# Attention layer with experts on one core: Q, K and V by seven block products in place of eight from the second batch on

## The chip, the core and the metric

The kernel runs on one core of a Trainium2 chip. The metric is device time in microseconds (us) of one execution; lower is better. The engines are named as in the profile: PE is TensorE, DVE VectorE, ACT ScalarE, POOL GpSimd, and SP the queue that only issues DMAs.

## The reference, cut to what matters

x is 4 batches of 1024 rows of 512. The layer is attention with 16 heads of width 128, a residual and a layer norm, then a router with 32 experts and a shared expert, a residual and a layer norm. The change is in the attention alone:

```python
qkv = einsum('bsh,hf->bsf', x, w_qkv)              # 512 -> 3 * 16 * 128
scores = einsum('bhqd,bhkd->bhqk', q, k) / sqrt(128)
probs = softmax(scores, axis=-1)
values = einsum('bhqk,bhkd->bhkd', probs, v)       # = v times the column sums of probs
out = values @ w_o                                 # then layernorm(x + out)
```

The second einsum with probs has no sum over different rows of v: each key's row of v is multiplied by the column sum of the probabilities.

## The kernel before

There are 64 heads in all (4 batches by 16), M in the code. They are worked in 32 pairs, `pair(i)`; n is the head whose scores are made, and in the same eight steps t the projections of head n + 1 are made. Every float32 matrix is kept as a rounded part (HI) and a rest (LO), and a product is three passes, HI*HI, HI*LO and LO*HI. One matmul instruction takes a 128 x 128 weight and 512 columns.

- PE, step t: `scores(n, t)` is 6 matmuls into one of two score banks pairs; it waits for `act_e`, the exponential of step t-2. Then in steps 0 to 5 `project(n + 1, g)` makes one of six groups (Q, K and V, each in two halves of 512 columns), 12 matmuls each, into one of the two banks `p_g`. `spread` (4 matmuls) lies in step 2; in steps 6 and 7 lie two `out_tile` each (6 matmuls each), which multiply the previous pair's values with w_o.
- DVE, step t: `max_tile` (L1325) on the scores, then the extras (`lo_g` L1347, `lo_cs` L1354, `times_v` L1363, `lo_val` L1368, `add_y` L1375), then `add_tile` of the step before (L1332, L1340).
- ACT, step t: first the casts to HI that stand in that step (`hi_g` L936, `hi_w` L907, `hi_cs`, `hi_val`, `hi_wo`, `hi_x`), then `exp_tile` (L953).
- POOL: `lo_w` (L640), `lo_wo` (L645) and `lo_x` (L652), the rests of the weights and of the next batch's x, behind ACT's casts.
- SP: loads of the raw weights and of x pieces, each 256 KB.

Each engine runs its instructions in the written order, and semaphores alone tie the engines together. After the last pair come the router, the shared expert and the experts; the change leaves them as they are, but for the place where some of their inputs come from.

## Time and profile before

| | |
|---|---|
| median of 3 runs | 2753.79 us (2751.57 to 2754.13) |
| profiled execution | 2753.52 us, span 2751.8 us |
| granted TensorE clock, mean | 0.997 |
| PE busy | 2730.4 us, 99% |
| DVE busy | 2162.6 us, 79% |
| ACT busy | 1407.3 us, 51% |
| POOL busy | 655.0 us, 24% |
| DMA | 193.51 MB, mean 70 GB/s |

The span is the time from the first to the last instruction; the execution's own time is 1.7 us more. A busy share is a mean over the attention (up to about 2165 us) and the rest. Matmuls overlap each other, so their spacing is read from the starts in the timeline and not from the length of one.

### The profile page before, as it was taken

Reading aid. Unit: us, or ns where it says so; the run is one execution under the profiler, and the core shown is the slowest. Engines: PE = TensorE matmul, PEld = TensorE weight load, DVE = VectorE, ACT = ScalarE, POOL = GpSimd, SP = SyncE. Lnnn points to the kernel's source line nnn. Section 1 sums busy time; section 2 is a strip of 40 time slices with the busy share of each in tenths; the row PEclk is TensorE's granted clock in tenths of the full one; section 3 lists DMA queues with packets and bytes.
Section 4 is the critical chain, followed back from the end, with each engine's and each line's share of the span. In section 5 each row is a group of like instructions: output and inputs, shape, how many; then the busy total and the mean of one; then the engine's idle time right before and its main releaser. Section 6 shows DMA issues by size and latency. Waiting matters only on the chain.

```text
span 2751.8 us, 41729 instructions
## 1 busy us (share of the span) xinstructions
PE 2730.4 (99%) x13008; PEld 2262.2 (82%) x13008; DVE 2162.6 (79%) x3193; ACT 1407.3 (51%) x2501; POOL 655.0 (24%) x690
## 2 busy tenths in 40 slices
PE   9999999999999999999999999999999999999998
PEld 7888888888888888888888888888888788888887
DVE  5988888888888888888888888888888787533346
ACT  5555555566555555665555557555555532244434
POOL 2221112222111211222112212212221110266520
PEclk9999999999999999999999999999999999999999
DMA  3111111113111111131111112211111231288954
GB/s 119 39 35 35 37 34 34 34 34 115 35 34 34 34 35 41 33 112 35 35 38 34 34 34 65 80 38 34 34 34 35 85 119 42 88 251 248 256 161 153
DMA packets 209639, 193.51 MB, mean 70 GB/s; under 512 B 14620, under 2 KB 162076, under 8 KB 209552
## 3 DMA queue, kind: packets, MB, share of 16 engines
q1 hardware_dynamic: 199056, 180.47, 20.7%
q0 software_dynamic: 10496, 12.02, 2.3%
q8 instruction: 38, 0.62, 0.1%
q14 instruction: 49, 0.40, 0.0%
HBM read 166.41 MB, written 36.18 MB: 74 GB/s over the span
## 4 chain that ended last, share of the span: by engine, by line
PE 96%; DVE 3%; issue 1%; ACT 1%; DMA 0%; DVEq 0%; ACTq 0%
PE banks L1789 37%; PE banks L1804 25%; PE banks L1827 13%; PE banks L1711 6%; PE banks L1760 5%; PE banks L1773 3%; PE banks L1720 2%; PE banks L1814 2%; PE banks L1635 1%; PE banks L1747 1%; DVE colsum L1340 1%; PE banks L1688 0%; PE banks L1659 0%; DVE neg_max L1325 0%; DVE rows_b L1363 0%
## 5 line engine op out<-in xcount | busy, mean ns | idle before, releaser
L1789 PE MATMUL banks<-xt,w_sb 128*128 (+1 forms) x4608 | 1109.1, 390 | 6.6 <-DVE xt L1419 6.6
L953 ACT ACTIVATE rows_a<-banks,neg_max 128x1024 f32<-128x1024 f32 x512 | 572.4, 1118 | 891.1 <-DVE neg_max L1325 890.7
L1789 PEld LDWEIGHTS banks<-xt,w_sb 128*128 128x128 f32 x4608 | 866.6, 188 | 187.4 <-POOL w_sb L640 6.6
L1325 DVE TENSOR_REDUCE neg_max<-banks 128x1 f32<-128x1024 f32 x512 | 625.9, 1222 | 282.5 <-PE banks L1804 279.6
L1804 PE MATMUL banks<-qk 128*128 128x512 f32 x3072 | 780.5, 390 | 0.5 <-ACT rows_a L953 0.5
L1804 PEld LDWEIGHTS banks<-qk 128*128 128x128 f32 x3072 | 576.9, 188 | 121.5 <-ACT rows_a L953 1.7
L1340 DVE SCALAR_TENSOR_TENSOR colsum<-rows_a,inv,colsum 128x1024 f32<-128x1024 f32 x448 | 586.8, 1310 | 18.8 <-DVE inv L1332 1.5
L640 POOL TENSOR_TENSOR w_sb<-raws,w_sb 128x512 fp32r<-128x512 f32 x192 | 257.9, 1343 | 1197.8 <-ACT w_sb L907 1197.8
L1827 PE MATMUL banks<-wo_sb,val 128*128 128x512 f32 x1536 | 372.1, 391 | 0.6 <-DVE y_sb L1375 0.6
L1827 PEld LDWEIGHTS banks<-wo_sb,val 128*128 128x128 f32 x1536 | 285.9, 188 | 67.3 <-DVE y_sb L1375 8.0
L645 POOL TENSOR_TENSOR wo_sb<-wo_raw,wo_sb 128x512 fp32r<-128x512 f32 x64 | 96.7, 1512 | 415.1 <-ACT wo_sb L913 415.1
L1711 PE MATMUL banks<-xt 128*128 128x512 f32 x768 | 184.4, 396 | 0.4 <-DVE rows_c L1304 0.4
L936 ACT ACTIVATE qk<-banks 128x512 fp32r<-128x512 f32 x256 | 152.7, 597 | 58.9 <-PE banks L1789 58.9
L1347 DVE SCALAR_TENSOR_TENSOR qk<-banks,qk 128x512 fp32r<-128x512 f32 x256 | 174.4, 681 | 5.6 <-ACT qk L936 5.6
L1711 PEld LDWEIGHTS banks<-xt 128*128 128x128 f32 x768 | 144.4, 190 | 31.0 <-issue 0.9
L1375 DVE TENSOR_TENSOR y_sb<-y_sb,banks 128x512 f32<-128x512 f32 x256 | 163.9, 680 | 4.1 <-PE banks L1827 4.0
L907 ACT CAST w_sb<-raws 128x512 fp32r<-128x512 f32 x192 | 118.1, 615 | 2.0 <-DMA raws<-in_w_qkv 2.0
L704 POOL DMA_INDIRECT acc_rows<-rows_b,who x64 | 94.1, 1471 | 87.1 <-DMA acc_rows<-rows_b,who 43.7
L880 ACT ACTIVATE rows_b<-banks,slot_w 80x512 f32<-80x512 f32 x64 | 43.6, 684 | 124.4 <-PE banks L1773 78.7
L1368 DVE TENSOR_TENSOR val<-rows_b,val 128x1024 fp32r<-128x1024 f32 x64 | 100.9, 1577 | 0.9 <-ACT val L947 0.9
L652 POOL TENSOR_TENSOR xt<-raws,xt 128x128 f32 (+1 forms) x128 | 80.7, 662 | 83.4 <-ACT xt L921 83.4
L1320 DVE TENSOR_TENSOR ehb<-ehf,ehb 128x320 fp32r<-128x320 f32 x32 | 15.7, 492 | 106.2 <-ACT ehb L875 106.2
(191 smaller groups left out, 2279.9 us busy)
## 6 DMA issues: line engine op xcount, KB each, us to landing
raws<-in_w_qkv SPq DMA_DIRECT2D x192, 256.0 KB, 2.9
wo_raw<-in_w_o SPq DMA_DIRECT2D x64, 256.0 KB, 2.8
y_sb<-in_x SPq DMA_DIRECT2D x32, 256.0 KB, 4.0
raw_own<-in_w_gate SPq DMA_DIRECT2D x16, 512.0 KB, 5.5
raw_own<-in_w_up SPq DMA_DIRECT2D x16, 512.0 KB, 5.7
raw_own<-in_w_down SPq DMA_DIRECT2D x16, 512.0 KB, 7.0
raws<-in_xT SPq DMA_DIRECT2D x25, 256.0 KB, 3.0
x_wide<-y_sb SPq DMA_DIRECT2D x24, 256.0 KB, 3.6
```

The lines of the kernel that those rows point to most:

```text
L640: pool.tensor_tensor(w_sb[:, LO, r], w_raw[:, r], rounded(w_sb[:, HI, r]), ALU.subtract)\
L936: act.activation(qk[:, par, r, HI, at], p_g[:, g % 2], ACT.Copy, scale=SCALE if r == Q else 1.0).then_inc(act_g, 1)
L953: act.activation(ex[:, t % 2], p_s[:, t % 2], ACT.Exp, bias=neg_max[:, t % 2], accum_out=rowsum[:, t % 2]).then_inc(act_e, 1)
L1325: dve.tensor_reduce(neg_max[:, t % 2], p_s[:, t % 2], AX_X, ALU.max, negate=True)\
L1340: dve.scalar_tensor_tensor(out=colsum[:], in0=ex[:, t % 2], scalar=inv[:, t % 2], in1=colsum[:], op0=ALU.mult, op1=ALU.add).then_inc(dve_p, 1)
L1347: dve.scalar_tensor_tensor(out=qk[:, par, r, LO, at], in0=p_g[:, g % 2], scalar=SCALE if r == Q else 1.0, in1=rounded(qk[:, par, r, HI, at ...
L1375: dve.tensor_tensor(y_sb[:, j], y_sb[:, j], p_o[:, j % 2], ALU.add).then_inc(dve_y, 1)
L1711: ins = pe.matmul(p_f(f % 2, r), s_gu[:, a, k, at], parts[:, PARTS_OF[u], b, k], start=(k == 0 and (a, b) == PASSES[0]), stop=(k == KC - 1 ...
L1760: ins = pe.matmul(expert_hidden(e, r)[:, ic * C_SLOTS:(ic + 1) * C_SLOTS], gate_up_of(e)[:, r, k, cols(ic)], exT[:, e % 2, k], start=(k == ...
L1789: ins = pe.matmul(p_g[:, g % 2], w_sb[:, a, r, c], xt_part(batch_par, b, c, half * NB, NB), start=(c == 0 and (a, b) == PASSES[0]), stop=( ...
L1804: ins = pe.matmul(p_s[:, t % 2, keys], qk[:, par, Q, a, at], qk[:, par, K, b, keys], start=((a, b) == PASSES[0]), stop=((a, b) == PASSES[-1]))
L1827: ins = pe.matmul(p_o[:, j % 2], val2[:, r, a, at], wo_sb[:, r, b], start=(r == 0 and (a, b) == PASSES[0]), stop=(r == 1 and (a, b) == PAS ...
```

## The change

**What it does.** A product of a matrix of 2 x 2 blocks with another is made from seven block products of sums of blocks (Strassen's method in Winograd's form). The blocks are two of the weights' columns (Q and K of a head, or V of two heads) by two halves of the depth 512, and two halves of depth by two halves of a batch's 1024 rows. A block product is `multiply`: 6 matmuls. Seven of them replace four groups of 12.

- In the first batch (pairs 0 to 7, `plain_head`) the projections are made as before. Beside it the sums for the later batches are made: per pair three sets of weights (`land_w`, `scale_new_w`, `combine_w`, `hi_new_w`, `low_w`, `store_w`), seven blocks of 256 words in two parts, and a piece of the next batch's x (`land_x`, `combine_x`, `hi_new_x`, `low_x`, `store_x_form`). They are stored in device memory. All the sets pass through one place in SBUF, `w_new`.
- From head 16 on (`quick`, and the second half of `turnover`, pair 7) a set of seven weights is read back per product: three per pair, each in two loads (`load_values`, `load_even`, `load_odd`) that POOL issues, 128x2048 and 128x1536 words, 1 MB and 0.75 MB. At a batch's end seven x blocks, 7 MB, are read back too (`load_x_form`).
- The results of the seven products are put together by ACT (`keep_q`, `keep_v`: a copy of the bank), DVE (`sum_q`, `sum_v`: bank plus a tile in SBUF) and POOL (`sum_q`, `sum_v`: two tiles in SBUF). `lo_q` and `lo_val` go to POOL; `lo_g` and `hi_w`, `lo_w` end with the first batch.

The lines of it that matter for the order (ACT in the first batch, SP at the start and at the end of a plain pair, POOL and PE in a quick one):

```diff
+        def land_w(first, second, count):
+            on_sp.wait_ge(out_w_form, 16 * count)
...
+        def store_w(at, count):
+            on_sp.wait_ge(pool_new_w, count + 1)
...
+        def plain(i):
...
+            land_piece(b, i)
+            if is_first(i):
+                land_w((Q, 1), (K, 1), 1)
+            store_w(n + 1, 3 * i + 1)
+            land_w((V, n), (V, n + 1), 3 * i + 2)
+            load_w(n + 3, n + 3)
+            store_w(H + i, 3 * i + 2)
+            store_piece(b, i)
+            land_w((Q, n + 2), (K, n + 2), 3 * i + 3)
+            store_w(n + 2, 3 * i + 3)
+            land_w((Q, n + 3), (K, n + 3), 3 * i + 4)
...
+        def scale_new_w(count):
+            on_act.wait_ge(in_new_w, 64 * (count + 1))
...
+        def plain_head(i, s):
...
+                if s == 0 and t == 0:
+                    scale_new_w(3 * i + 1)
+                if s == 1 and t == 4:
+                    scale_new_w(3 * i + 3)
+                if s == 0 and t == 1:
+                    hi_new_w(3 * i + 1)
...
+                if s == 1 and t == 6:
+                    hi_new_w(3 * i + 3)
+                exp_tile(n, t)
...
+        def load_values(b, i, part):
+            on_pool.wait_ge(pe_g, G * H + FORMS * (2 * i + 1 - H) + LOADS[part][1])
+            load_w_form(H + i - PB * b, part)
...
+        def multiply(bank, k):
+            for c in range(2):
+                for a, b in PASSES:
+                    ins = pe.matmul(p_g[:, bank], w_form[:, k, a, c], x_form[:, k, b, c],
+                                    start=(c == 0 and (a, b) == PASSES[0]), stop=(c == 1 and (a, b) == PASSES[-1]))
...
+        def product_v(i, k):
+            m = 2 * i + 1
+            on_pe.wait_ge(in_w_form[LOAD_OF[k]], 16 * (w_load(i, "values") + 1))
...
         def scores(n, par, t, quickly=True):
+            if t in (0, 4) and quickly:
+                on_pe.wait_ge(pool_w, 3 * H + 8 * (n - H) + (6 if t == 0 else 8))
+        def first_head(i):
...
+                if t == 0:
+                    product_q(i, 0, 0)
+                    product_q(i, 0, 1)
...
+                if 4 <= t <= 6:
+                    product_v(i, 2 * (t - 4))
+                    product_v(i, 2 * (t - 4) + 1)
```

**ACT at the start.** These rows stand around the first exponentials, those of head 0; L953 before and L1317 now is `exp_tile`. Before:

```order
L932 COPY v_sb<-banks 128x512 x2
L907 CAST w_sb<-raws 128x512
L953 ACTIVATE rows_a,rowsum<-banks,neg_max 128x1024
L936 ACTIVATE qk<-banks 128x512
L953 ACTIVATE rows_a,rowsum<-banks,neg_max 128x1024
```

Now, at the same place (L1226 is `scale_new_w`, L1230 `hi_new_w`, L1240 `hi_new_x`):

```order
L1296 COPY v_sb<-banks 128x512 x2
L1215 CAST w_form<-raws 128x512
L1226 ACTIVATE xt_words<-xt_words 128x2x256
L1230 CAST xt<-xt_words 128x7x256
L1240 CAST xt<-xt_words 128x7x128
L1226 ACTIVATE xt_words<-xt_words 128x2x256
L1317 ACTIVATE rows_a,rowsum<-banks,neg_max 128x1024
L1300 ACTIVATE qk<-banks 128x512
L1230 CAST xt<-xt_words 128x7x256
L1317 ACTIVATE rows_a,rowsum<-banks,neg_max 128x1024
```

Ahead of the first exponential now stand the whole of set 0, piece 0 of x, and the scaling of set 1.

**POOL in a quick pair.** These rows are the begin of pair 9; L859 is `sum_q`, L874 `lo_val`, L846 `lo_q`, L772 a weight load, L765 `lo_wo`. Before, POOL's work of a pair was six L640, two L645 and one piece of x.

```order
L859 TENSOR_TENSOR qk_words<-qk_words,raws 128x512
L874 TENSOR_TENSOR val<-rows_b,val 128x1024
L846 TENSOR_TENSOR qk<-qk_words,qk 128x512
L772 DMA w_form<-w_forms 128x2048
L859 TENSOR_TENSOR qk_words<-qk_words,raws 128x512
L765 TENSOR_TENSOR wo_sb<-wo_words,wo_sb 128x2x512
L859 TENSOR_TENSOR qk_words<-qk_words,raws 128x512
L772 DMA w_form<-w_forms 128x1536
```

The first L772 here loads the weights of the first four V products, which PE wants in step 4 of this head.

**PE in a quick pair.** These rows are steps 0 to 4 of the first head; L2366 is `scores`, L2317 a block product (6 matmuls, or 12 for two), L2376 `spread`:

```order
L2366 MATMUL banks<-qk 128x512 x6
L2317 MATMUL banks<-xt,w_form 128x512 x12
L2366 MATMUL banks<-qk 128x512 x6
L2317 MATMUL banks<-xt,w_form 128x512 x12
L2366 MATMUL banks<-qk 128x512 x6
L2317 MATMUL banks<-xt,w_form 128x512 x6
L2376 MATMUL banks<-cs,ones 128x512 x4
L2366 MATMUL banks<-qk 128x512 x6
L2317 MATMUL banks<-xt,w_form 128x512 x12
L2366 MATMUL banks<-qk 128x512 x6
L2317 MATMUL banks<-xt,w_form 128x512 x12
```

Before, a group of 12 stood in each of steps 0 to 5; now steps 0 to 7 hold two, two, one, two products of Q and K and then two, two, two, one of V.

## Rows read from the trace of the kernel before

**Rows 1.** The page: the chain that ended last, by engine and by line.

```profile
PE 96%; DVE 3%; issue 1%; ACT 1%; DMA 0%; DVEq 0%; ACTq 0%
```

**Rows 2.** Timeline of PE in a middle pair: start us, us, instructions.

```profile
1299.96 1.52 PE L1804 MATMUL banks<-qk 128*128 128x512 f32 x6
1301.32 2.88 PE L1789 MATMUL banks<-xt,w_sb 128*128 x12
1304.04 1.07 PE L1814 MATMUL banks<-cs,ones 128*128 128x512 f32 x4
1304.95 1.52 PE L1804 MATMUL banks<-qk 128*128 128x512 f32 x6
1306.31 2.88 PE L1789 MATMUL banks<-xt,w_sb 128*128 x12
1309.03 1.52 PE L1804 MATMUL banks<-qk 128*128 128x512 f32 x6
```

**Rows 3.** Busy time in a pair's 67.2 us: PE, PEld, DVE, ACT, POOL.

```profile
1299.00:1366.20 67.20, 67.20 (x297) 55.47 (x297) 57.53 (x73) 35.18 (x61) 13.66 (x13) 1.00 0.12 35
```

**Rows 4.** Timeline of DVE and ACT in the same pair, steps 3 and 4.

```profile
1306.51 1.23 DVE L1325 TENSOR_REDUCE neg_max<-banks 128x1 f32<-128x1024 f32 x1 [0.64 <-PE banks L1804]
1307.65 0.68 DVE L1347 SCALAR_TENSOR_TENSOR qk<-banks,qk 128x512 fp32r<-128x512 f32 x1
1307.77 1.12 ACT L953 ACTIVATE rows_a<-banks,neg_max 128x1024 f32<-128x1024 f32 x1 [2.42 <-DVE neg_max L1325]
1308.25 1.27 DVE L1363 TENSOR_TENSOR rows_b<-v_sb,banks 128x512 f32<-128x512 f32 x2
1308.79 0.19 ACT L953 ACTIVATION_READ_ACCUMULATOR rows_a<-banks,neg_max 128x1 f32 x1
1309.63 1.28 DVE L1340 SCALAR_TENSOR_TENSOR colsum<-rows_a,inv,colsum 128x1024 f32<-128x1024 f32 x1
```

**Rows 5.** Timeline of the start of the kernel: SP, PE and ACT.

```profile
18.33 4.09 SPq L500 DMA_DIRECT2D y_sb<-in_x  x8
26.73 0.62 ACT L907 CAST w_sb<-raws 128x512 fp32r<-128x512 f32 x1
28.87 1.12 ACT L953 ACTIVATE rows_a<-banks,neg_max 128x1024 f32<-128x1024 f32 x1 [1.51 <-DVE neg_max L1325]
34.21 1.52 PE L1804 MATMUL banks<-qk 128*128 128x512 f32 x6
```

**Rows 6.** Groups by line and shape over the span: xcount, busy us, mean ns.

```profile
L640 POOL TENSOR_TENSOR w_sb<-raws,w_sb 128x512 fp32r<-128x512 f32 x192 | 257.9, 1343 | 1197.8 <-ACT w_sb L907 1197.8
L743 POOL TENSOR_TENSOR qk<-raw_own,qk 128x1024 fp32r<-128x1024 f32 x2 | 4.8, 2376 | 8.8 <-ACT qk L901 8.8
L907 ACT CAST w_sb<-raws 128x512 fp32r<-128x512 f32 x192 | 118.1, 615 | 2.0 <-DMA raws<-in_w_qkv 2.0
L947 ACT CAST val<-rows_b 128x1024 fp32r<-128x1024 f32 x64 | 67.0, 1047 | 1.4 <-DVE rows_b L1363 1.4
```

**Rows 7.** DMA issues: KB each, median us from issue to landing.

```profile
raws<-in_w_qkv SPq DMA_DIRECT2D x192, 256.0 KB, 2.9
out_rows<-y_sb SPq DMA_DIRECT2D x2, 1024.0 KB, 4.7
out_rows<-y_sb SPq DMA_DIRECT2D x2, 512.0 KB, 2.8
rows_a<-x_wide SPq DMA_DIRECT2D x3, 1024.0 KB, 5.0
x_wide<-dense POOLq DMA_DIRECT2D x8, 64.0 KB, 2.2
```

**Rows 8.** Timeline of DVE and POOL where both work: the same L1368 twice.

```profile
1303.26 1.22 DVE L1368 TENSOR_TENSOR val<-rows_b,val 128x1024 fp32r<-128x1024 f32 x1
1304.39 0.16 DVE L1332 RECIPROCAL inv<-rowsum 128x1 f32<-128x1 f32 x1
...
1315.51 1.30 POOL L640 TENSOR_TENSOR w_sb<-raws,w_sb 128x512 fp32r<-128x512 f32 x1 [3.45 <-ACT w_sb L907]
1315.81 2.08 DVE L1368 TENSOR_TENSOR val<-rows_b,val 128x1024 fp32r<-128x1024 f32 x1
```

**Rows 9.** PE's one pause in the attention, timeline, then windows with the clock.

```profile
2138.26 1.33 PE L1635 MATMUL banks<-ident,rows_c 128*128 128x128 f32 x8 [2.04 <-DVE xt L1171]
2139.24 2.91 PE L1804 MATMUL banks<-qk 128*128 128x512 f32 x6
2141.94 1.41 PE L1814 MATMUL banks<-cs,ones 128*128 128x512 f32 x4
...
2139.20:2142.00 2.80, 2.80 (x10) 2.22 (x9) 2.60 (x4) 2.13 (x4) 0.00 (x0) 0.51 0.00 0
```

More of the change, by code:

```diff
@@ L1422, in _ @@
             lo_g(0, 0, g)
-        pairs(dve, pair)
+        pairs(dve, plain, turnover, quick)
         add_tile(M - 1, T - 1)
-        add_y(PAIRS - 1, 6)
         add_y(PAIRS - 1, 7)
@@ new lines, in plain_head @@
+        def plain_head(i, s):
+            n = 2 * i + s
+            for t in range(T):
+                scores(n, s, t, quickly=False)
+                g = group_at(i, t)
+                if g is not None:
+                    project(n + 1, 1 - s, g)
+                if t == 2 and not (is_first(i) and s == 0):
+                    if not is_first(i):
+                        on_pe.wait_ge(dve_y, T * (i - 1) if s == 0 else T * (i - 1) + 4)
+                    spread(n - 1)
+                if t >= 6 and not is_first(i):
+                    if t == 6:
+                        on_pe.wait_ge(dve_v, 2 * n)
+                    out_tile(i, 4 * s + 2 * (t - 6))
+                    out_tile(i, 4 * s + 2 * (t - 6) + 1)
```

946 lines of the change are left out of this document (721 added, 225 removed).

## The prediction

> **What bounds the kernel now.** I read the chain that ended last first: 96% of it is PE [rows 1]. Then a middle pair in PE's timeline: scores start at 1299.96, the group at 1301.32, so 6 matmuls take 1.36 us; the next scores after group and spread start at 1304.95, those after at 1309.03, 4.08 us for 18 matmuls [rows 2]. One matmul costs 0.2267 us and nothing lies between them. A pair has 296, which is 67.1 us. In the same stretch DVE is busy 57.5 us, ACT 35.2, POOL 13.7 [rows 3]. So PE sets the time of every pair, DVE has some 9.6 us of room, POOL more than 50. The timeline of DVE and ACT gives the slack of a step: the scores that start at 1304.95 are reduced from 1306.51, their exponential runs from 1307.77 to 1308.98, 4.0 us after the scores' start [rows 2, 4]. PE wants it two steps later, at 8.16 us. An exponential may be some 4.1 us late before PE stands.
>
> **What the change takes off PE.** Four groups of 12 matmuls become seven of 6: 6 fewer for each of 48 heads' Q and K and for each of 24 pairs' V, 432 matmuls. At 0.2267 us that is **-97.9 us**, all of it on the path as long as PE stays packed. A quick pair is 278 matmuls, 63.0 us.
>
> **Prices of the new operations.** POOL: 512 columns 1.29 us uncontended (the row of L640 in rows 8; its mean is 1.34), 1024 columns 2.38 [rows 6, 8], so 2.1 ns per column: 256 columns 0.74, 1792 columns 4.05. ACT: 512 columns 0.615, 1024 columns 1.05 [rows 6], so 1792 columns 1.7. A store of 1.75 MB: 512 KB took 2.8 us and 1024 KB 4.7 [rows 7], so estimated 6.7 (1.5 to 1.9 for each further 512 KB). Four loads of 128 KB: one of 256 KB lands in 2.9 us, and the fourth issue comes later by some 1.3, so 4.2. A load of 1 MB that POOL issues: the row has 64 KB in 2.2 us there and 1024 KB in 5.0 on SP [rows 7]; I take 5.1. The operation is in no trace; its bounds are 4.0 and 8.
>
> By the Trainium skill ("DMA: Bandwidth & Descriptors", Anatomy of one DMA, SWDGE path) such a load takes an estimated 2.0 us and the bytes at 436 GB/s, 4.4 us for 1 MB. By it the wait priced below would be 0.7 us shorter in each of 24 pairs, 17 us in all. The rows go before it, since they are of this kernel's own tiles, and no row here shows a large load from POOL.
>
> **The start.** Before, the first exponential starts at 28.87 and PE goes on without a gap [rows 5]. Now ACT's queue has set 0, piece 0 and the scaling of set 1 ahead of it. Laid end to end: loads of y occupy SP to 22.4 and their 2 MB must move first, set 0 lands near 29.5, scaling 0.6, four dependent POOL sums 3.3, cast 1.7, POOL's rest 4.05 (behind piece 0's sums) to 39.5, store to 46.5. Piece 0 (3584 rows of 256 B) is stored behind it, to 50; SP then lands piece 1 (its wait stands first) and set 1, to 57. The first exponential starts at 58, 29 us late; less the 4.1 of slack PE stands 25 us. Set 1's sums hold the second exponential in the same way for some 2 more. **+27 us**, and the clock: after PE's one pause of 2.04 us the next 6 matmuls took 2.7 us in place of 1.36, with a granted clock of 0.51, the 1.2 GHz level [rows 9]. 3.4 us at half rate cost 1.7. **+1.7**. Behind ACT here stand the exponentials and so all of PE and DVE; nothing else covers it.
>
> **Pairs 1 to 7.** All three sets of a pair pass through one place, so a set cannot land before the last is stored. The third set is cast in step 6 of the second head, 0.6 + 1.7 us behind its begin; then POOL 4.05, store 6.7, loads 4.2, scaling 0.6: set 4 is scaled 17.9 us after that step began. Step 0 of the next pair begins 8.16 after it and its exponential would start 2.8 later, at 10.96. It is 7.0 late, 2.9 more than the slack. The four sums then hold the second exponential (4.5 us with one DVE operation in between): another 1.4. **+4.3 us in each of 7 pairs, +30**. If the store and loads are 3 us quicker, 1.3 a pair; if DVE and the other transfers hold them, 7. The other two sets fit: their casts come later than their loads.
>
> **Quick pairs: the V weights.** In the first head POOL does the first sum (at 5.4 to 6.7 us of the pair, behind `keep_q` of product 1), then `lo_val`. That needs ACT's `hi_val`, which stands in step 2 behind the exponential of step 1 (to 8.3), a copy and a cast of 0.6 each and itself 1.05: 10.6. `lo_val` 2.4 to 13.0, then DVE's sum takes its turn (1.0), `lo_q` to 15.3, and only then the load is issued; it lands at 20.5. PE has three steps of 4.08, less 0.45 in step 2, and 1.36 of scores: it wants product 0 of V at 17.2. It stands **3.3 us, in 24 pairs +79**. Its cover would be later work of PE, but the order is fixed and the next scores are behind it. The second load lands by 28.5, when PE, now late, wants it. I do not count the clock's fall here: 1.7 us each time, 41 in all, is kept for the range, for the pause is near the only one that the trace shows.
>
> **Quick pairs: DVE and POOL.** DVE loses eight L1347 (0.60 by start to start, [rows 4]) and two L1368 (1.13, [rows 8]), and gets nine sums of 0.60: 57.5 - 4.8 - 2.3 + 5.4 = 55.8 us, and the contention of POOL. POOL gets per pair twenty operations of 512 columns, three of 1024, 2.1 for a piece's rest and four small: 25.8 + 7.1 + 2.1 + 1.8 = 36.8 us, and six issues of about 0.8. L1368 took 1.22 alone and 2.08 where POOL's L640 was under way, until which it did nothing [rows 8]. I call those DVE operations that read two tiles of SBUF exclusive against POOL: per pair 14 L1340, 2 L1337 and 2 L1354, 21.9 us. Both together need 58.7 of the 66 us, so it fits but DVE is often late by one POOL operation. Head for head that shows where slack is small: K's last `lo_q` must be done before the next pair's scores. ACT casts it behind the exponential of step 6, 0.6 us into step 7, POOL needs 1.3, and step 7 is but 2.72 long: 0.8 of slack. I take a wait of 0.3 us in 24 pairs, **+7**; bounds 0 and 1.5.
>
> The rule against this change is in the Trainium skill ("SBUF — State Buffer", two separate sides): the port pair that VectorE and GpSimd share is an exclusive lock, held for the whole instruction. By that rule the sum of both engines' lock time, not either's busy share, is the measure; it is the rival of VectorE's port below. The trace agrees in L1368's 2.08 us.
>
> **Batch openings and the end.** At the ends of batches 1 and 2 (pairs 15 and 23) 8.75 MB are issued by POOL from about 33 us of the pair, and PE wants the last of them 19 us later; at the 3.1 us per MB that the 1024 KB row leaves after 2 us of latency they take 27. Products spread over the steps cover most: **+6 each, 12**. The 14 small POOL operations of a norm stand ahead of the K chain three times, 2 each, **+6**. 4 MB for the shared expert are issued late in the last pair: **+3**.
>
> **The sum.** -97.9 + 27 + 1.7 + 30 + 79 + 7 + 12 + 6 + 3 = +67.8. From the profiled execution's own 2753.5 that is 2821; it stands 0.3 under the median, so **2822 us** against 2753.8.
>
> **Rivals.**
> - *The loads are in time (faster).* If the V weights land by 17.2 + 0.5 us and the sets' circle is 3 us quicker, what is left is -97.9 + 28.7 + 9 + 12 + 7 + 12 = -29: 2725; without the openings' waits 2710. For it: PE has no other new dependency in step 4. Against it: `hi_val` at 10.6 and `lo_val` at 13.0 stand on measured rows. It decides where the wait is under 0.5 us per pair. Chance 0.20.
> - *VectorE's port.* If POOL and DVE get in each other's way more than their turns fit, each exclusive DVE operation waits half a POOL operation, 18 x 0.65 = 11.7 us, DVE needs 67.5, and with in-order waits of ACT on POOL's results 70 per pair: 24 x (70 - 67.1) + 59 + 21 = +150, 2903. For it: 58.7 of 66 us. Against it: DVE catches up while PE stands. Chance 0.12.
> - *Half clock after each wait.* As the forecast, and each 3.3 us pause costs 1.7 more: 2863. For it rows 9, against it that a shorter pause may not lower the clock. Chance 0.20.
> - *It cancels.* Waits of 0.8 us per quick pair: within 0.2%. Chance 0.04.
> - The forecast: 0.44.
>
> 0.2% (5.5 us) is about what a measurement of this kernel can tell from no change. Faster is the first rival, 0.20; same 0.04; the rest slower, 0.76. The range goes to the first rival's half and to the port's case: 2722 to 2900. The forecast's own range is 2785 to 2850.
>
> **What would show it.** In the changed profile: 12576 matmuls; the first exponential (L1317) near 58 us; in pairs 1 to 7 ACT's L1226 waiting for a DMA and PE's scores for ACT, pairs of about 71.4 us; in quick pairs a pause of L2317 in step 4 with a DMA as its releaser, issued by L772, pairs of about 66.6; clock under 1 after it or not. Wrong would be: no pause at step 4 (then faster), or DVE's L1340 with a mean well over 1.5 us and DVE without idle time (then the port).

## The result and the profile after

The changed kernel takes **2995.05 us** (median of 4 runs, 2992.64 to 2996.57) against 2753.96 for the kernel before in the same rounds: a ratio of 1.088 (1.086 to 1.090), 241 us slower. The forecast was 2822 with a range up to 2900: right in its sign, 173 us short in its size.

The page of the changed kernel: the chain that ended last by engine, then three groups of operations (xcount, busy us and mean ns, idle time before them and its releaser):

```profile
PE 47%; issue 22%; POOL 10%; DVE 10%; DMA 6%; ACT 3%; SPq 2%; DVEq 1%; POOLq 0%; ACTq 0%
...
L1774 DVE SCALAR_TENSOR_TENSOR colsum<-rows_a,inv,colsum 128x1024 f32<-128x1024 f32 x448 | 903.2, 2016 | 17.6
L2317 PE MATMUL banks<-xt,w_form 128*128 128x512 f32 x3024 | 787.4, 409 | 103.4 <-DMA w_form<-w_forms 79.0
L2366 PE MATMUL banks<-qk 128*128 128x512 f32 x3072 | 791.8, 394 | 45.4 <-ACT rows_a L1317 35.1
```

PE's share of the chain fell from 96% [rows 1] to 47%; L1774 is DVE's `add_tile`, whose mean was 1310 ns before over the same 448 operations. PE waited 79.0 us for loads of weights, the number that the forecast has for it, and yet that is a third of the loss only.

Where the 241 us lie is read from the starts of `spread` (L2376), which stands once in every head at the same place. The table gives the time from the spread in one pair's second head to that in the next pair's, named by the first of the two:

| | before | after | sum of the difference |
|---|---|---|---|
| first spread | 65.5 | 92.7 | +27.2 |
| pair 0 | 61.8 | 78.2 | +16.5 |
| pairs 1 to 7 | 67.2 | 74.3, the last 76.7 | +52 |
| pairs 8, 16, 24 (norm of the batch before) | 67.6 | 85.3, 85.4, 84.5 | +52 |
| the 20 other distances between quick pairs | 67.2, the last 64.4 | 70.9 to 71.0 in nine, 69.8 to 74.3 in the others | +87 |
| the rest | | | +6 |

A middle quick pair, the same views as [rows 2 to 4]. First the windows: the pair, PE's pause in it, and what follows the pause (length, then busy us of PE, PEld, DVE, ACT, POOL, the granted clock, DMA share, GB/s). Then the timelines of PE, POOL and DVE:

```profile
1504.30:1575.20 70.90, 65.78 (x280) 53.03 (x279) 65.57 (x73) 35.40 (x58) 43.58 (x34) 0.98 0.35 102
1543.18:1546.74 3.56, 0.16 (x1) 0.00 (x1) 3.56 (x1) 0.20 (x1) 3.56 (x3) 1.00 0.69 249
1546.74:1551.20 4.46, 4.46 (x13) 3.52 (x14) 4.46 (x4) 0.59 (x1) 1.58 (x2) 0.62 0.56 176
```

```profile
1541.82 1.52 PE L2366 MATMUL banks<-qk 128*128 128x512 f32 x6
1546.74 4.59 PE L2317 MATMUL banks<-xt,w_form 128*128 128x512 f32 x12 [3.40 <-DMA w_form<-w_forms]
```

```profile
1531.86 1.29 POOL L859 TENSOR_TENSOR qk_words<-qk_words,raws 128x512 f32<-128x512 f32 x1 [3.03 <-ACT qk_words L1271]
1536.52 2.42 POOL L874 TENSOR_TENSOR val<-rows_b,val 128x1024 fp32r<-128x1024 f32 x1 [3.37 <-ACT val L1311]
1538.88 2.29 POOL L846 TENSOR_TENSOR qk<-qk_words,qk 128x512 fp32r<-128x512 f32 x1
1541.11 0.57 POOL L772 DMA_DIRECT2D w_form<-w_forms  x1
1541.70 1.30 POOL L859 TENSOR_TENSOR qk_words<-qk_words,raws 128x512 f32<-128x512 f32 x1
1542.96 2.34 POOL L765 TENSOR_TENSOR wo_sb<-wo_words,wo_sb 128x1024 fp32r<-128x1024 f32 x1
1545.26 1.25 POOL L859 TENSOR_TENSOR qk_words<-qk_words,raws 128x512 f32<-128x512 f32 x1
1546.46 0.57 POOL L772 DMA_DIRECT2D w_form<-w_forms  x1
1547.05 1.29 POOL L846 TENSOR_TENSOR qk<-qk_words,qk 128x512 fp32r<-128x512 f32 x1
```

```profile
1541.86 7.58 DVE L1774 SCALAR_TENSOR_TENSOR colsum<-rows_a,inv,colsum 128x1024 f32<-128x1024 f32 x1
1549.36 1.21 DVE L1759 TENSOR_REDUCE neg_max<-banks 128x1 f32<-128x1024 f32 x1
...
1551.87 1.29 DVE L1774 SCALAR_TENSOR_TENSOR colsum<-rows_a,inv,colsum 128x1024 f32<-128x1024 f32 x1
```

Read it so. The load that PE wants was issued at 1541.11, behind `lo_val` (L874) and `lo_q` (L846); PE stands 3.56 us more than the usual spacing, and the 12 matmuls behind it take 4.44 us in place of 2.72, at a granted clock of 0.62, a mix of the 1.2 and 2.4 GHz levels. The pair's 278 matmuls are 63.0 us; 3.56 of pause, some 1.7 of half clock, three small pauses (0.84, 0.63, 0.73) and crumbs give 70.9. Below, `add_tile` takes 7.58 us where the same operation takes 1.29 some ten microseconds later: it starts 0.16 us behind POOL's L859 and ends at 1549.44, 1.10 us after the last of four POOL operations (L859, L765, L859, L846) has ended. DVE is busy 65.57 us of the pair, and the work that the forecast counted for it is 55.8; the 9.8 between are waits inside its operations.

The half clock is no term by itself. The next pair has the same late load, but full clock behind it (a window), and then a wait of PE for ACT, whose exponential had stood 7.22 us for DVE's `neg_max`, which stands behind an `add_tile` of 7.58 us:

```profile
1617.29:1620.15 2.86, 2.86 (x12) 2.36 (x13) 2.86 (x1) 0.00 (x0) 1.93 (x3) 1.00 0.53 122
```

```profile
1617.29 3.02 PE L2317 MATMUL banks<-xt,w_form 128*128 128x512 f32 x12 [3.05 <-DMA w_form<-w_forms]
1620.15 1.52 PE L2366 MATMUL banks<-qk 128*128 128x512 f32 x6
1623.24 3.02 PE L2317 MATMUL banks<-xt,w_form 128*128 128x512 f32 x12 [1.57 <-ACT raws L1286]
```

```profile
1621.51 1.11 ACT L1317 ACTIVATE rows_a<-banks,neg_max 128x1024 f32<-128x1024 f32 x1 [7.22 <-DVE neg_max L1759]
```

Both pairs are 70.9 us. Of the 24 pauses for V's weights (3.0 to 4.3 us each by the starts) 19 were followed by half rate, which cost 1.5 to 3.0 us. Behind the five others stood a wait for ACT of 1.3 to 1.7 us instead. So under the late load and the half clock lay VectorE's hold, hidden by them.

The first batch. PE at the start, and ACT's wait there; then a plain pair, in which DVE's `add_tile` meets POOL's rest of a whole weight set (L817, 1792 columns):

```profile
57.95 2.93 PE L2366 MATMUL banks<-qk 128*128 128x512 f32 x6 [24.11 <-ACT rows_a L1317]
```

```profile
56.17 0.63 ACT L1226 ACTIVATE xt_words<-xt_words 128x512 f32<-128x512 f32 x1 [19.70 <-DMA xt_words<-in_w_qkv]
56.71 1.10 ACT L1317 ACTIVATE rows_a<-banks,neg_max 128x1024 f32<-128x1024 f32 x1
```

```profile
261.13 4.04 POOL L817 TENSOR_TENSOR xt<-xt_words,xt 128x1792 fp32r<-128x1792 f32 x1 [2.94 <-ACT xt L1230]
```

```profile
261.56 4.69 DVE L1774 SCALAR_TENSOR_TENSOR colsum<-rows_a,inv,colsum 128x1024 f32<-128x1024 f32 x1
266.18 1.27 DVE L1838 TENSOR_TENSOR y_sb<-y_sb,banks 128x512 f32<-128x512 f32 x2
```

```profile
266.91 3.64 PE L2389 MATMUL banks<-wo_sb,val 128*128 128x512 f32 x9 [2.63 <-DVE y_sb L1838]
```

The start is as forecast (a pause of 24.1 us where 25 was said, first exponential at 56.7 where 58 was). In the plain pair PE stands for `add_y`, not for the exponential.

### The profile page after: what moved, and what is told of

Its sections match the earlier page's. It is cut to its first block, busy times and chain, and to the rows that moved or that the text cites. A ratio compares the mean times of both kernels' runs of the same rounds, so it can differ in the third digit from the quotient of the medians.

```text
span 2993.4 us, 40911 instructions
## 1 busy us (share of the span) xinstructions
PE 2738.7 (91%) x12576; PEld 2222.5 (74%) x12576; DVE 2432.8 (81%) x3169; ACT 1450.4 (48%) x2461; POOL 1579.5 (53%) x1322
## 4 chain that ended last, share of the span: by engine, by line
PE 47%; issue 22%; POOL 10%; DVE 10%; DMA 6%; ACT 3%; SPq 2%; DVEq 1%; POOLq 0%; ACTq 0%
PE banks L2317 13%; PE banks L2366 9%; PE banks L2230 5%; PE banks L2389 5%; PE banks L2279 5%; PE banks L2292 3%; DVE neg_max L1759 3%; PE banks L2239 3%; DMA w_form<-w_forms 3%; POOL xt L817 2%; DMA xt_words<-in_w_qkv 2%; SPq L515 1%; DVE y_sb L1838 1%; DMA w_forms<-xt 1%; DVE colsum L1774 1%
## 5 line engine op out<-in xcount | busy, mean ns | idle before, releaser
L1317 ACT ACTIVATE rows_a<-banks,neg_max 128x1024 f32<-128x1024 f32 x512 | 572.3, 1118 | 922.8 <-DVE neg_max L1759 922.3
L1774 DVE SCALAR_TENSOR_TENSOR colsum<-rows_a,inv,colsum 128x1024 f32<-128x1024 f32 x448 | 903.2, 2016 | 17.6
L2317 PE MATMUL banks<-xt,w_form 128*128 128x512 f32 x3024 | 787.4, 409 | 103.4 <-DMA w_form<-w_forms 79.0
L2366 PE MATMUL banks<-qk 128*128 128x512 f32 x3072 | 791.8, 394 | 45.4 <-ACT rows_a L1317 35.1
L2317 PEld LDWEIGHTS banks<-xt,w_form 128*128 128x128 f32 x3024 | 593.1, 198 | 254.0 <-issue 73.8
L2366 PEld LDWEIGHTS banks<-qk 128*128 128x128 f32 x3072 | 585.3, 191 | 173.1 <-ACT rows_a L1317 36.3
L846 POOL TENSOR_TENSOR qk<-qk_words,qk 128x512 fp32r<-128x512 f32 x192 | 302.0, 1574 | 239.2 <-ACT qk L1248 238.7
L859 POOL TENSOR_TENSOR qk_words<-qk_words,raws 128x512 f32<-128x512 f32 x192 | 252.0, 1313 | 152.2 <-DVE qk_words L1815 77.7
L2308 PE MATMUL banks<-xt,w_form 128*128 128x512 f32 x1152 | 286.1, 399 | 20.3 <-DVE qk L1781 13.7
L2308 PEld LDWEIGHTS banks<-xt,w_form 128*128 128x128 f32 x1152 | 220.4, 193 | 73.4 <-DVE qk L1781 11.2
L874 POOL TENSOR_TENSOR val<-rows_b,val 128x1024 fp32r<-128x1024 f32 x48 | 123.4, 2571 | 85.1 <-ACT val L1311 84.6
L870 POOL TENSOR_TENSOR v_sb<-v_sb,raws 128x512 f32<-128x512 f32 x96 | 141.3, 1491 | 0.0
L840 POOL TENSOR_TENSOR xt<-xt_words,xt 128x896 fp32r<-128x896 f32 x24 | 52.1, 2172 | 156.9 <-ACT xt L1240 156.9
L1248 ACT CAST qk<-qk_words 128x512 fp32r<-128x512 f32 x192 | 119.8, 624 | 26.1 <-POOL qk_words L859 25.8
L760 POOL TENSOR_TENSOR w_form<-raws,w_form 128x512 fp32r<-128x512 f32 x48 | 79.8, 1663 | 89.6 <-ACT w_form L1215 89.6
```

The source lines that it names most:

```text
L846: pool.tensor_tensor(qk[:, par, r, LO, at], qk_words[:, par, r, LO, at], rounded(qk[:, par, r, HI, at]), ALU.subtract).then_inc(pool_w, 1)
L859: pool.tensor_tensor(to, to, stash[:, kept], ALU.add).then_inc(pool_w, 1)
L1317: act.activation(ex[:, t % 2], p_s[:, t % 2], ACT.Exp, bias=neg_max[:, t % 2], accum_out=rowsum[:, t % 2]).then_inc(act_e, 1)
L1774: dve.scalar_tensor_tensor(out=colsum[:], in0=ex[:, t % 2], scalar=inv[:, t % 2], in1=colsum[:], op0=ALU.mult, op1=ALU.add).then_inc(dve_p, 1)
L2308: ins = pe.matmul(p_g[:, g % 2], w_sb[:, a, r, c], xt[:, 0, b, c, half * NB:half * NB + NB], start=(c == 0 and (a, b) == PASSES[0]), stop= ...
L2317: ins = pe.matmul(p_g[:, bank], w_form[:, k, a, c], x_form[:, k, b, c], start=(c == 0 and (a, b) == PASSES[0]), stop=(c == 1 and (a, b) == ...
```

## The experiments

Each is one profiled run, on a chip that ran the kernel before at 2751.6 to 2755.4 beside it. The four runs of the changed kernel lie 3.9 us apart, so a difference of some 5 us is read from the pairs and not from the time. "Pair" is the usual distance of spreads in the stretch named. POOL's code of the first head of a quick pair is the ground of most edits:

```python
sum_q(m, 1, "P1")
lo_val(n - 2, 0)
lo_q(m, 1, Q, 0, 1)
load_values(b, i, 0)
sum_q(m, 1, "P5")
lo_wo(i)
sum_q(m, 1, "P5 of K")
load_values(b, i, 1)
lo_q(m, 1, K, 0, 2)
lo_q(m, 1, K, 1, 3)
```

### The late load, and what stands behind it

**e1_values_first.**

```diff
             sum_q(m, 1, "P1")
+            load_values(b, i, 0)
             lo_val(n - 2, 0)
             lo_q(m, 1, Q, 0, 1)
-            load_values(b, i, 0)
```

> The first V load is issued before lo_val and lo_q in all 24 quick pairs; nothing else changes. Theory 'late load': the pause of 3.56 us in step 4 and the half clock behind it (1.7) go, 24 x 5.26 = 126 us, so 2995 becomes about 2869. Rival 'VectorE held': the add_tile that takes 7.58 us in each quick pair keeps the exponential of step 4 late, PE stands one or two steps later, and at most half is won: 2930 or more, with a new pause of PE whose releaser is ACT or DVE in steps 5 and 6.

**2944.2 us**, -51 where the load's wait and its half clock are worth 126. The pause in step 4 is gone in every pair, and the pair falls from 70.9 to 69.8 only. Three steps later PE stands 2.9 us before its first `out_tile`. The view names no releaser, but POOL's second `lo_val`, which `out_tile` waits for, ends at 1537.26, 0.10 us before PE starts. Then PE stands for DVE's `add_y`, behind an `add_tile` of 7.01 us:

```profile
1537.36 1.61 PE L2389 MATMUL banks<-wo_sb,val 128*128 128x512 f32 x6 [2.74 <-issue]
...
1542.73 1.65 PE L2389 MATMUL banks<-wo_sb,val 128*128 128x512 f32 x6 [1.04 <-DVE y_sb L1838]
```

```profile
1534.91 2.35 POOL L874 TENSOR_TENSOR val<-rows_b,val 128x1024 fp32r<-128x1024 f32 x1
1537.21 3.77 POOL L870 TENSOR_TENSOR v_sb<-v_sb,raws 128x512 f32<-128x512 f32 x3
```

```profile
1535.06 7.01 DVE L1774 SCALAR_TENSOR_TENSOR colsum<-rows_a,inv,colsum 128x1024 f32<-128x1024 f32 x1
```

So the load's wait was real, and it covered another of about its own length. Of the 5.3 us a pair that the theory gave, the plain quick pairs got 1.1; the norm pairs, which have several waits, got 6 us each.

**e2_wo_later** and **e12_both**: `lo_wo(i)` moved from between the two sums P5 to behind K's second `lo_q`, alone and with the edit of e1.

> Only lo_wo (1024 columns, 2.4 us) is moved from between the two sums P5 to behind K's lo_q, in the quick pairs. By 'VectorE held by operations of GpSimd that follow each other without a gap' the 7.58 us of add_tile become about 5.2; by 'it takes turns' nothing changes in them. PE's time: by 'late load' nothing moves, 2990 to 2998, since the load is issued ahead of it; by 'VectorE held' some 1 to 2 us a pair are won, 2950 to 2970.

> Both edits. By 'late load' alone it equals e1_values_first, about 2869. If VectorE's held operation is what stands behind the load, this run is better than e1_values_first by more than e2_wo_later was better than 2995: then about 2870 here and 2930 there.

**3080.3** and **2977.1 us**: 85 slower than the changed kernel, and 33 slower than e1. Both expectations were wrong in the time. The operation that was held for four POOL operations is held for three in 21 pairs (5.3 us in place of 7.6), as expected. But in the changed kernel `lo_wo` stood ahead of 5.03 us in which POOL waits for ACT's cast of K, and was covered by them; the edit puts it behind that wait, ahead of the sum P3 and the second `lo_val`. PE, which still stands 3.4 us on the mean for the late load, now stands mostly 3.6 before its first `out_tile` too, where it was 0.73 in the middle pair, and in 17 pairs a second `add_tile` is held for 7.0 us, behind that `lo_val` and three sums. The pair is 75.1. An operation that is moved out of the shadow of a wait costs its whole length.

**e5_gaps**: e1 with waits of POOL on its own last result.

```diff
             sum_q(m, 1, "P5")
+            on_pool.wait_ge(pool_w, 3 * H + 8 * (m - H) + 3)
             lo_wo(i)
+            on_pool.wait_ge(pool_wo, i)
             sum_q(m, 1, "P5 of K")
...
             lo_val(n - 1, 1)
+            on_pool.wait_ge(lo_v, n)
             sum_v(i, "P5")
+            on_pool.wait_ge(pool_v, 4 * (i - PB) + 2)
             sum_v(i, "P5 of both")
...
```

> e1_values_first with six waits of GpSimd on its own last result, so that no five of its operations follow each other without a gap; no work is added or moved. Theory 'VectorE loses its turn only while GpSimd's operations follow without a gap': the add_tile of 7.0 us (19 of them in that run, behind lo_val and three sums) is at most 3.7 in all 24 pairs, PE's waits for add_y behind it (1.2 and 0.85 us) go, pairs of 69.8 become 67.5 to 68.5, and the time 2895 to 2920. Rival 'GpSimd simply has the port while it has work': the operation stays at 7 us and the time at 2944. PE's 2.74 us before the first out_tile stay in both, for they wait for lo_val itself.

**2939.5 us.** The mechanism holds: of the 592 DVE operations of 1024 columns whose inputs lie in SBUF (L1774, L1771, L1788, L1831) 25 waited for more than one POOL operation in the changed kernel, 21 in e1, and one here, in the last pair, which the edit leaves alone. The waits inside these operations sum to 284 us, against 350 in e1. The price was wrong: pairs of 68.4 in about half of them and 69.6 to 69.9 in the others, and 5 us in all. PE's pause for `lo_val` (2.6 to 2.9) was left, and in the longer pairs half clock followed it (1.6 to 1.7).

**e6_lo_val**: e1 with both `lo_val` on DVE, behind `add_tile` of steps 2 and 6.

> e1_values_first with both lo_val of a quick pair given back to VectorE, which did them before the change (behind add_tile of steps 2 and 6). GpSimd loses 4.7 us a pair, VectorE gets 2.4. Theory 'GpSimd's queue is too late for what PE wants in step 7': the pause of 2.74 us before out_tile and what follows it go, pairs of 69.8 become 65 to 66, time 2840 to 2860. Rival 'VectorE is the bound by now': its 2.4 us more are all paid or half of the gain is lost, 2900 or more.

**2940.9 us**, the rival's case. PE's pause before `out_tile` is down to 0.7, and another of 2.2 us with 1.7 of half clock stands in step 4, for a sum of DVE (L1812). The reason is in DVE's timeline: `lo_val`, 1.2 us of work, took 3.41 behind POOL's `lo_wo`.

```profile
1511.69 3.33 POOL L765 TENSOR_TENSOR wo_sb<-wo_words,wo_sb 128x1024 fp32r<-128x1024 f32 x1
```

```profile
1512.69 3.41 DVE L1828 TENSOR_TENSOR val<-rows_b,val 128x1024 fp32r<-128x1024 f32 x1
```

**e10_lo_val_first**: e5 with POOL's second `lo_val` ahead of `sum_v` P1 and of the even weights' load.

> e5_gaps with GpSimd's second lo_val of a pair ahead of sum_v P1 and of the even weights' load, 2.8 us sooner. By 'PE's first out_tile waits for that lo_val' its pause (2.6 us, in every second pair with 1.6 of half clock) goes: pairs of 68.4 and 69.9 become 65.5 to 66.5, 2855 to 2875. By 'VectorE is short of time all through the pair' the pause comes back elsewhere, and pairs stay above 68, 2920 or more.

**2892.9 us.** The pause went, the pair is 66.9: between the two expectations. This is the first order whose quick pair is shorter than the 67.2 of before. DVE is busy 61.49 of 66.9 us there, and what PE still waits is four pauses of 0.5 to 1. From pair 14 to 15 and from 22 to 23, the ends of batches, the time is 72.4 and 72.5: PE stands 3.9 us for weights whose load is behind the x loads, with 1.7 of half clock.

### POOL's work itself

**e8_short_sums**: the sums and `lo_val` on 8 columns.

```diff
-            at = slice(half * NB, half * NB + NB)
+            at = slice(half * NB, half * NB + 8)
             on_pool.wait_ge(act_v, 4 * (i - PB) + read)
```

> The changed kernel, in which GpSimd's twelve sums and two lo_val of a quick pair are done on 8 columns in place of 512 and 1024 (so Q, K and V are not the reference's from the second batch on); every wait, load and rest stays in its place. GpSimd's work of a quick pair falls from some 37 to 17 us. Theory 'GpSimd's own work makes the quick pairs long, by its queue and by the port': pairs of 70.9 become 63.5 to 65, 24 x 6.5 = 155 us less, about 2840. Rival 'the seven loads of a pair and PE's clock': half of the excess stays, pairs of 67 or more, 2900.

**2789.9 us**, -205, more than the theory asked. One window over a quick pair, as above:

```profile
1415.00:1478.40 63.40, 63.29 (x280) 52.10 (x279) 55.31 (x72) 35.63 (x58) 24.15 (x34) 1.00 0.38 114
```

PE is packed at full clock, DVE's 55.31 us are the 55.8 of the forecast, all loads, casts and waits are in their old places, and the load of V's weights is in time. The norm pairs fell from 85.1 to 70.9 with all 15 small operations in them. Over their neighbours they are still 7.5 us. The kernel is 36 us slower than the one before, and the first batch alone costs 94 (below), so the matmuls' saving is there: the durations of POOL's operations, by its queue and by the port together, are the cause of nearly all of the quick pairs' loss.

**e9_more_pool**: the kernel before, with sums that nobody reads.

```diff
+        def more(i, burst):
+            for k in range(3 * burst, 3 * burst + 3):
+                on_pool.wait_ge(pool_tw, 18 * i + k + 1)
+                pool.tensor_tensor(rows_c[:, 3], rows_c[:, 3], rows_c[:, 3], ALU.add).then_inc(pool_tw, 1)
...
                     lo_w(n + 2, Q)
+                    more(i, 3 * s + 0)
```

> The kernel before the change, in which GpSimd makes 18 more sums of 512 columns per pair (three behind each rest of weights, each behind a wait for the last) that nothing reads; they add 23 us of GpSimd's work to its 13.7 and no wait to anybody. Theory 'the port alone does it': VectorE's 21 us of operations on two tiles of SBUF wait, L1340's mean rises from 1.31 to over 1.6 us, VectorE's 9.6 us of room are used and pairs of 67.2 become 68 or more, 2780 to 2840. Rival 'the port alone is covered, it needs results that somebody waits for': L1340's mean rises as much, pairs stay at 67.2, 2754 to 2762. I take the rival for likelier.

**2792.7 us**: the theory, not the rival that I took for likelier. No other engine waits for the new operations in the attention, and in no pair does PE stand for POOL; yet the pair is 68.5 in the first three batches (67.6 in the last):

```profile
L1350 DVE SCALAR_TENSOR_TENSOR colsum<-rows_a,inv,colsum 128x1024 f32<-128x1024 f32 x448 | 691.9, 1544 | 18.8 <-DVE inv L1342 1.5
```

```profile
1342.53 5.12 POOL L677 TENSOR_TENSOR rows_c<-rows_c 128x512 f32<-128x512 f32 x3
```

```profile
1343.76 1.87 DVE L1350 SCALAR_TENSOR_TENSOR colsum<-rows_a,inv,colsum 128x1024 f32<-128x1024 f32 x1
...
1346.87 1.86 DVE L1350 SCALAR_TENSOR_TENSOR colsum<-rows_a,inv,colsum 128x1024 f32<-128x1024 f32 x1
```

```profile
1349.38 2.79 PE L1837 MATMUL banks<-wo_sb,val 128*128 128x512 f32 x11 [1.09 <-DVE y_sb L1385]
```

Two `add_tile` in a row are 0.6 longer than before; they make `add_y` late, and PE stands 1.25 us once in each pair of 68.5, though DVE had 9.6 us of room over the pair. The port by itself costs 1.3 us a pair for 23 us of POOL.

**e3_short_norm.**

```diff
-            link.step(pool.tensor_scalar(v, n_square[:, c % 2], 1.0 / D, EPS, ALU.mult, ALU.add))
-            rsqrt(v, a, g)
+            link.step(pool.tensor_scalar(g, n_square[:, c % 2], 1.0 / D, EPS, ALU.mult, ALU.add))
```

> The changed kernel with 2 small GpSimd operations per norm in place of 15 (the Newton steps are left out, so the norm of the first three batches is not the reference's). Theory 'the small operations ahead of K's chain cost more than a step's slack': the pairs of 85.3, 85.4 and 84.5 become about 72 (a quick pair of 70.9 and 1), 3 x 13 = 40 us less, 2955. Rival 'a batch's opening is dear for ACT's and VectorE's norm work': pairs 8, 16 and 24 keep 80 or more, 2980.

**2972.6 us**: pairs 8, 16, 24 are 77.5, 78.4, 76.5. About half of what they have over a quick pair (14.2) is the small operations' doing, 7.6 us; the other half is left. In the changed kernel they come in two bunches at each batch end, 5.0 to 6.0 us each: behind the first PE's scores stand 3.4 to 3.7 us for K's last rest, behind the second its `out_tile` 6.4 us for `lo_val`, and half clock follows both. In e8, with the small operations and without the long sums, it is also half that goes.

### The first batch

**e4_no_sets**: no `land_w`, `scale_new_w`, `combine_w`, `hi_new_w`, `low_w`, `store_w`.

> All weight sets of the first batch are left out (landing, scaling, sums, cast, rest and store, set 0 too); the quick pairs load words of w_qkv in their place, so the output is not the reference's. Pieces of x stay. By my account of the first batch: the start (27, of which the piece of x keeps a few us), pair 0 (16.5), pairs 1 to 7 (7.1 each, 50) go: -85 to -95, so 2900 to 2910, and its pairs are 67.2 us again. Rival 'the port, not the store': POOL's small sums and rests cost the same as the landing circle; they go too, so the sum is the same, but what is then left in a plain pair over 67.2 is owed to the pieces of x alone.

**2901.0 us**, -94.0. The first spread is at 65.0, pair 0 62.8, pairs 1 to 5 68.16 and pair 6 61.8: the account of the first batch is right in its sum, and the x pieces cost 1.0 a pair. The circle and POOL's hold on the port went together here, so the run does not tell them apart.

**e7_scale_later** and **e12_low_parts**, two single edits:

```diff
-                if s == 0 and t == 0:
+                if s == 0 and t == 2:
                     scale_new_w(3 * i + 1)
...
-                if s == 0 and t == 1:
+                if s == 0 and t == 3:
                     hi_new_w(3 * i + 1)
```

> The changed kernel with ACT's scaling of a pair's first set of weights in step 2 in place of 0 and its cast in step 3 in place of 1; no work is taken away. Theory 'the circle through the one place is late for ACT's place in the order': the set lands 5.2 us after ACT first wants it, two steps are 8.2, so the wait goes: pairs 1 to 7 become 68 to 69.5 in place of 74.3, 7 x 5.3 = 37 us; at the start the second set no longer holds the first exponential but the third, which gives 10 to 15 us more. 2940 to 2950. Rival 'the port and the traffic hold the first batch': nothing moves but the wait's place, 2980 or more.

```diff
-            pool.tensor_tensor(w_new[:, :, LO], w_new_words[:, :, LO], rounded(w_new[:, :, HI]), ALU.subtract)\
-                .then_inc(pool_new_w, 1)
+            for k in range(0, FORMS, 2):
+                at = slice(k, min(k + 2, FORMS))
+                ins = pool.tensor_tensor(w_new[:, at, LO], w_new_words[:, at, LO], rounded(w_new[:, at, HI]),
+                                         ALU.subtract)
...
```

> The changed kernel with the rest of a weight set (GpSimd, 1792 columns, 4.04 us in one operation) in four operations of 512, 512, 512 and 256 columns, each behind a wait for the last. Theory 'one long operation of GpSimd holds VectorE': the add_tile of 4.7 us behind it becomes one of at most 2.6, PE's pause of 2.6 us for add_y and the half clock behind it (1.8) go, pairs 1 to 7 fall from 74.3 to 70 to 72, time 2965 to 2980. Rival 'the circle through the one place is all': the rest takes 0.5 us longer now, the next set comes that much later, and the time is 2995 to 3000.

**2983.2** and **3010.0 us**. In the first, 8 us of pair 0 went and the pairs are 71 to 77, with PE's 3.0 us for `add_y` still there. In the second that pause is gone from the pair looked at, and PE stands 4.8 us for the exponential, for the set has come later:

```profile
358.90 2.48 PE L2372 MATMUL banks<-qk 128*128 128x512 f32 x6 [4.63 <-ACT rows_a L1323]
```

```profile
357.13 0.63 ACT L1232 ACTIVATE xt_words<-xt_words 128x512 f32<-128x512 f32 x1 [11.11 <-DMA xt_words<-in_w_qkv]
```

**e15_both_waits**: both at once, `lo_wo` ahead of the rest.

> The changed kernel with both edits of the first batch that gave little or nothing alone: the scaling and cast two steps later (e7_scale_later, -12 us) and the rest of the weights in four operations (e12_low_parts, +15 us), with lo_wo ahead of that rest. Theory 'two waits of about the same length, of which each covers the other' (PE for add_y behind VectorE, held by the long rest; PE for the exponential behind ACT, late for the next set): together they give what neither gave, pairs 1 to 6 become 68 to 70 in place of 74.3, 2995 - 8 (pair 0) - 6 x 5 = 2950 to 2965. Rival 'the gains are those of each alone': 2995 - 12 + 15 = 2998, or 2985 with w_o sooner.

**3009.4 us**: the time is not what the theory gave. One of a pair's two distances from spread to spread is now nearly as short as it can be (33.8 us), and the other, 40.5 to 42, has two pauses for ACT's exponential, 2.3 and 2.4 us with half clock. The second stands behind ACT's cast of the second set. The first stands behind its cast of w_o:

```profile
285.72 1.04 ACT L1226 CAST wo_sb<-wo_words 128x1024 fp32r<-128x1024 f32 x1 [4.84 <-DMA wo_words<-in_w_o]
```

SP issues that load behind the landing of a set. ACT waits for it seven times, 26.8 us in all, and never in the first batch of the changed kernel or of e12_low_parts. So the pause travels and the pair stays at 74 to 76, but the run does not settle the theory: it took two waits away and opened a third.

**e11_places** and **e14_places_again**: the sets five steps apart, set 0 behind the first exponential; then w_o's load mended.

> The changed kernel with the first batch's weight sets put elsewhere in ACT's and GpSimd's order, by some five steps of 4.08 us each from one set to the next, with set 0 begun behind the first exponential; no work is added or taken away. By my account of the first batch: start (28), pair 0 (16.5) and pairs 1 to 7 (7 each) are waits for a set that comes later than its place, so they fall to 3, 3 and 1 to 2 each: 2995 becomes 2905 to 2925. If the port or the store's traffic were behind them, they stay: 2960 or more.

> e11_places with SP's loads of the next pair's weights and of w_o ahead of the store and the landing of the pair's last set; there w_o came 11.7 us after ACT wanted it. Theory 'the order of the waits in SP and ACT made the first batch long': the wait for w_o goes, pairs of 80 become 69 to 72, the start stays at 8 us over the kernel before; 2930 to 2950. Rival 'one place for all sets is too slow in any order': pairs stay above 74, 2970 or more.

**3025.4 us**: my own order made SP load w_o only behind the store of the last set, and ACT's cast of it blocked the exponentials:

```profile
276.21 1.04 ACT L1243 CAST wo_sb<-wo_words 128x1024 fp32r<-128x1024 f32 x1 [11.70 <-DMA wo_words<-in_w_o]
```

**2970.4 us** with that mended. The start fell from 92.7 to 74.7, and the pairs to 72 to 73.5; but the last set is later, and pair 6 to 7 takes 83.0.

**e17_short_store**: e12_low_parts, and a seventh of the store.

> e12_low_parts with the store of a weight set cut to its first seventh, 256 KB in place of 1.75 MB (the quick pairs load words of w_qkv, so the output is not the reference's); the landing, the scaling, the sums, the cast and the rest stay. A store takes 5.7 us now and would take some 2.8. Theory 'three sets through one place take longer than a pair, so their whole circle is the bound of the first batch and no order of the queues helps': the circle gets 3 x 2.9 = 8.7 us shorter, pairs 1 to 6 of 75.4 become 67.5 to 69, the start 3 us less; 3010 - 3 - 7 x 7 = about 2955. Rival 'the port': VectorE's holds in the first batch are the same as in e12_low_parts, pairs stay over 73, 2990 or more.

**2970.1 us**, -40: about halfway. The store fell from 5.7 to 2.0 us and the pair from 75.5 to 71.6; the first spread came 8 us sooner. What stands in a pair now is four pauses of 0.7 to 1.1 (3.7 us), like those of e10, three behind DVE and one behind ACT. So some 4 us of the pair's 8 are owed to the circle of the three sets through one place, by the store's length or by its traffic; for the other 4 no run took VectorE's holds away.

### All together

**e13_together** (e10, e14, e12_low_parts, `lo_val` and `lo_wo` in halves, norm and loads moved) and **e16_all_mild** (e10, e15, the even weights ahead of x).

> All that helped: e10_lo_val_first, e14_places_again, e12_low_parts, and besides GpSimd's lo_val and lo_wo in two halves, the norm's small operations in the first head before sum P3, and the even weights' load ahead of the next batch's x. Added up from the runs: 2893 - 19 (start) - 8 (pair 0) - 35 (pairs 1 to 7 to about 70) - 17 (batch ends) - 15 (norm) = about 2800, 2770 to 2830. If VectorE's time is the limit that is left, the quick pairs stay at 66.9 and it is 2810 or more; if the long single operations were its trouble, they fall to 65 and it is 2770 or less.

> e10_lo_val_first (2893) with the edits of e15_both_waits and the even weights' load ahead of the next batch's x. If the causes add up: -37 (first batch) - 17 (batch ends) = 2839; 2830 to 2855. If the first batch's waits cover each other still: 2870 or more.

**2903.2** and **2904.7 us**, both worse than e10 alone. e16's batch ends gained (pairs 14 and 22 from 72.4 and 72.5 to 68.3 and 68.8) and its first batch lost: it has e15's waits for w_o's load (28.1 us in seven), and pair 6 to 7 takes 80.5. In e13 the sets of the first batch end later, and the first loads of the seven products wait for them:

```profile
607.31 2.93 PE L2369 MATMUL banks<-xt,w_form 128*128 128x512 f32 x6 [16.51 <-DMA w_form<-w_forms]
```

The best version found, e10, is 139 us slower than the kernel before. No run beat it.

## Why the prediction was wrong, point by point

- **432 matmuls fewer, -97.9**: right. 12576 matmuls, and e8's pairs of 63.4 show that they can be had.
- **The start, +27 and +1.7**: right (+27.2 in all, a pause of 24.1, released by L1317 at 57.8, with 2.4 of half clock).
- **Pairs 1 to 7, +4.3 each**: size and path wrong. The set is scaled at about the time worked out (350.0, 17.0 us after PE's step 6 began; forecast 17.9), and ACT's L1226 waits 5.2 to 7.3 us for it. But in the pairs PE hardly stood for the exponential (once, 2.2 us, near the batch's end): it stood for DVE, 2.8 us with 1.7 of half clock for `add_y`, behind the `add_tile` of 4.69 us, and 1.5 for `lo_g` (L1781), behind holds of 2.69 and 3.23. The late set was covered by them. Pair 0 cost 16.5, where nothing was put, the others 7.1 and the last 9.5. "The other two sets fit" took the circle for 20 us each time: from store to store the three take 26.6, 27.7 and 20.1 us. The rest (3.96 to 4.44) and the store (5.7) are no longer than forecast, but one of the three landings takes 7.5 us where 4.2 was said, 5.3 of them for its four issues. Forecast 59 for the whole first batch, measured 96 (e4: 94).
- **V's weights, +79**: right, 3.3 a pause on the mean of 24, and the page has 79.0. **But as a term of a sum it failed**: e1 took it away and got 51 with its half clock, for other waits lay under it.
- **The clock's fall, kept out of the sum**: it came behind 19 of the 24 pauses, some 42 us together, where the range had 41. The reason given ("the pause is near the only one that the trace shows") spoke for it: 3.3 is longer than the 2.04 of [rows 9]. In the sum it would have been no better: where it did not come, the pair was no shorter. Only the nine cases of 2.7 to 3.0 us have longer pairs, by about 1.
- **K's last rest, +7**: no such wait in the middle pair; in its place three others of 0.6 to 0.8, 2.2 together, behind DVE, ACT and POOL's second `lo_val`. The wait itself came at the three batch ends, 3.4 to 3.7 us each.
- **Batch ends, +12**: 1.9 and 3.4 in the changed kernel (pairs 14 and 22 are 72.8 and 74.3), and 5.5 and 5.6 once PE was better packed (e10), where 6 each was forecast. Right price, partly covered by other waits.
- **The norm, +6**: 14.2 over a quick pair, three times, 43. Its chained operations of 0.28 us from start to start are 4.2 us, and 5.0 to 6.0 where DVE takes turns, not 2. They come twice at each batch end, not once, and the second bunch stands ahead of `lo_val` and not of K's chain.
- **The step that failed** is the sentence "Both together need 58.7 of the 66 us, so it fits but DVE is often late by one POOL operation", priced at 0.3 us a pair. The waits inside DVE's operations are 9.8 us a pair, near the 11.7 that the rival of VectorE's port has, and that rival gives a pair of 70 where 70.9 was measured. The rival had a chance of 0.12 and 2903 us, and even it lacks the first batch's 37 and most of the norm's 43. A sum of lock time under 100% says that the work fits in the mean; e9 has DVE busy for 61.5 of 68.5 us and PE still stands 1.25 us in each of these pairs, since the slack is that of two steps and the holds come in bunches.

The evidence against the chance given was in [rows 8]: an operation that grew from 1.22 to 2.08 us beside a single POOL operation. POOL was to go from eight operations of 512 columns a pair to twenty, and three of double length.

What stays open: how the 7.5 us that e8 takes off a quick pair divide between POOL's queue and the port (e9 gives 1.3 for the port in another setting; no run has one without the other), what the half of the norm's excess is that stays without its small operations, and how much of a plain pair's excess the late sets and VectorE's holds have each, since they cover each other.

## What to carry to other kernels

When a change gives an idle engine work beside a busy one, do not ask whether their busy times fit in the span; count the waits inside the busy engine's operations and compare the worst bunch with the slack of the one or two steps that the bound engine allows. A wait of 79 us on the page is no promise of 79 us: look at what comes next on the waiting engine once it is gone, and test with the operations made short (e8) before any order is mended. A single place that several sets pass through is a circle: add up its whole round, with the waits in the issuing queue, before its parts are set against the steps. And before an operation is moved in a queue, look for the wait that covers it where it stands (e2).
